# Making the high half of the gated product one column chunk later in the FFN stages

## The chip, the cores and the metric

The kernel runs on one core of one Trainium2 chip. The metric is the device time of one execution in microseconds (us), median over runs.

## What is computed

The reference is a "macaron" block on x of shape 2 x 2048 x 512 (4096 tokens), all in float32:

```
x = x + 0.5 * ffn(layernorm(x))
x = x + attention(layernorm(x))      # 16 heads of 32, causal
x = x + 0.5 * ffn(layernorm(x))

ffn(x):  w_gu, w_down = dequantised 4-bit weights (groups of 128, float16 scales)
         gate, up = x @ w_gu.T          # 1408 columns each
         h = silu(gate) * up
         y = h @ w_down.T
         return y / sqrt(mean(y*y) + 1e-6)
```

The same FFN weights are used twice.

## The kernel before

The program runs these stages: FFN, then for each of the two batches QKV projection, attention and output projection, then the FFN again. Only the FFN stages are touched by the change.

An FFN stage (class `Ffn`, `ph` 0 or 1) walks over 8 token tiles of 512 tokens (tt), and in each over 11 units (i), blocks of 128 of the 1408 gated columns. The units are numbered through, n = 11 tt + i. A unit has four chunks c, the four blocks of 128 of the 512 model columns. For each chunk two groups of two matmuls are made, up (u = 1) and gate (u = 0). The input is kept as a sum of two float16 halves x1 and x2, and each group is one weight block times x1 and times x2. The 4-bit weights have a scale for each group of 128 input columns, so each chunk's product must be scaled by itself. That is why every chunk is taken out of PSUM ("evac") rather than accumulated there:

- chunk 0, both halves: ScalarE writes `acc[u]` (a scaled copy);
- chunk 1, up: ScalarE writes a scaled copy to `tmp`, and GpSimd adds it to `acc[1]` (signal `added`);
- chunk 1, gate, and chunks 2 and 3: VectorE adds the scaled product to `acc[u]` (scalar_tensor_tensor). Chunk 2's up half has to wait for `added`.

The eight groups of a unit take their banks from a ring of four (`Ring`), so a group waits for the evacuation of the group four places before it in the ring. A "turn" (the transposition of 128 columns of the next tile's normalised input, four transposes) takes a place in the same ring.

At the end of a unit ScalarE makes silu(gate) ("silu", line 615). GpSimd multiplies it by the up half to h (lines 854 to 862; in the first tile of the first stage VectorE does this). In the next unit, h is split: ScalarE rounds it to float16, h1, the high half (line 621), and GpSimd subtracts to get h2, the low half (line 875). The down projection takes three matmuls for each 128 tokens (h1 x wd high, h1 x wd low, h2 x wd high) into four other banks Y. Its matmuls are issued LAG = 9 chunks behind, so those of unit n-1 begin in unit n+1, chunk 1.

The order of all of this is one list written by the generator `order` (line 316). Each engine's function (`ffn_pe`, `ffn_act`, `ffn_dve`, `ffn_pool`, `ffn_sp`) walks the same list and issues its own share in that order, waiting on semaphores for what it needs. An engine's queue is thus in list order, and an instruction that waits holds up all that stands behind it on its engine.

Into the list `slots` places further work: statistics of the next tile ("stat", "isd": small steps of 128x4 on VectorE in units 1 to 4), "apply" on ScalarE in units 5 and 6, the finish of the tile before ("square" on ScalarE in units 2 and 3, "rms" on VectorE in units 5 and 6, "last" on ScalarE and GpSimd in units 7 and 8), and in the units 7 to 10 the turns. The event "down" of a tile's last unit also makes ScalarE copy Y out of PSUM, which falls in the next tile's units 1 and 2. In the first tile of the first stage the weights are decoded as well: VectorE's bit operations ("decode"), TensorE's transposes, ScalarE's evacuations ("weight"), GpSimd's scaling.

In the trace nearly every instruction bears the line of a helper: L97 matmul, L100 transpose, L103 activation, L106 tensor_tensor, L109 tensor_scalar, L112 scalar_tensor_tensor. They are told apart by their operands: on ScalarE "sb<-sb 128x512 f32<-" is silu, "sb<-ps,sb" or "sb<-pp,sb" an evacuation (with its scale), "sb<-sb 128x512 f16<-" is h1, and "sb<-pp" without a scale operand a copy.

Of the kernel before, what the change touches and what calls it, by code (L numbers as in the profile page):

```python
# [281 lines left out]
class Ffn:  # L282
# [33 lines left out]
    def order(self):  # L316

        deq, ph = self.deq, self.ph
        if deq:
            yield "scales",  # L320
            yield from self.norm_v(0)
            yield from self.norm_a(0)
            yield "decode", 0, 99
            yield "scaled", 0
            yield "scaled", 1
            yield "decode", 1, 99
        for c in range(KC):
            yield "turn", 0, c
        yield "load", 1
        if deq:  # L330
            for m in range(3):
                yield "weight", m
            yield "vectors",
        for tt in range(NT):
            first = deq and tt == 0
            slots = self.slots(tt)
            for i in range(IC):
                n = tt * IC + i
                for c in range(KC):
                    for u in (1, 0):  # L340
                        yield "group", tt, i, c, u
                    for u in (1, 0) if c == 0 else (0, 1):
                        yield "evac", tt, i, c, u
                    if c == 0 and n:
                        yield "h1", n - 1
                    if c == 1 and n:
                        yield "h2", n - 1
                    d = 4 * n + c - LAG
                    if d >= 0:
                        yield "down", d // 4, d % 4  # L350
                    yield from slots.get((i, c), ())
                    if first and i + 1 < IC and c < 3:
                        yield "weight", 3 * (i + 1) + c
                    if first and c == 0 and i == 0:
                        yield "decode", 2, 99
                    if first and c and i + 3 < IC:
                        yield "decode", i + 3, 5 if c < 3 else 99
                    if tt + 1 < NT:
                        if c == 1 and i >= IC - 4 and not first:
                            yield "turn", tt + 1, i - IC + 4  # L360
                        if i == IC - 1 and first:
                            yield "turn", tt + 1, c
                if n == 0:
                    yield "settle",
                yield "silu", n
                if i == IC - 1:
                    yield "residual", tt
                    if tt + 2 < NT:
                        yield "load", tt + 2
                if tt == NT - 1 and i == 1 and ph == 0:  # L370
                    yield "ahead",
                if deq and tt in (2, 3) and i >= 3 and i - 3 + 8 * (tt - 2) < IC:
                    yield "keep", i - 3 + 8 * (tt - 2)
        n = NT * IC
        yield "h1", n - 1
        yield "h2", n - 1
        for d in range(4 * n - LAG, 4 * n):
            yield "down", d // 4, d % 4
        if ph:
            yield from self.finish_a(NT - 1) + self.finish_v(NT - 1) + self.finish_y(NT - 1)  # L380
# [1571 lines left out]
```

How the kernel before makes its waits and increments, by code:

```python
    def wait_ge(self, sem, value):  # L86
        if self.e is not None:
            assert value > 0, sem.name
            if self.seen.get(sem.name, 0) < value:
                self.seen[sem.name] = value
                self.e.wait_ge(sem, value)
# [145 lines left out]
def rsqrt_dve(e, p, out, x, scale, eps, mult, w, done=None, key=None):  # L237
    V = p.V
    v, g, t = w[:, 0, :], w[:, 1, :], w[:, 2, :]
    e.wait_ge(*V.now())
    e.tensor_scalar(v, x, scale / mult ** 2, eps / mult ** 2, ALU.mult, ALU.add).then_inc(*V.up())
    yield
    e.wait_ge(*V.now())
    e.tensor_scalar(t.bitcast(I32), v.bitcast(I32), 1, None, ALU.logical_shift_right).then_inc(*V.up())
    yield
    e.wait_ge(*V.now())
    e.tensor_scalar(g.bitcast(I32), t.bitcast(I32), -1.0, float(0x5F3759DF), ALU.mult, ALU.add).then_inc(*V.up())
    yield
    for n in range(3):
        e.wait_ge(*V.now())
        e.tensor_tensor(t, g, g, ALU.mult).then_inc(*V.up())
        yield
        e.wait_ge(*V.now())
        e.scalar_tensor_tensor(t, t, -0.5, v, ALU.mult, ALU.mult).then_inc(*V.up())
        yield
        e.wait_ge(*V.now())
        e.scalar_tensor_tensor(out if n == 2 else g, t, 1.5, g, ALU.add, ALU.mult).then_inc(
            *(done.up(key) if done and n == 2 else V.up()))
        yield
# [2 lines left out]
def norm_dve(e, p, ready, done, key, scale=1.0, eps=1e-5):  # L263
    V = p.V
    st, mv, rs, w = p.st, p.mv, p.rs, p.w4
    for tb in range(4):
        e.wait_ge(*ready)
        e.bn_stats(st[:, tb, :], p.xb[tb][:, :]).then_inc(*V.up())
        yield
```

## Time and profile before

| | |
|---|---|
| median of 3 runs | 2636.36 us (2633.56 to 2638.26) |
| the profiled execution | 2637.86 us, of which the span is 2636.0 |
| busy, share of the span | TensorE 95%, VectorE 72%, ScalarE 57%, GpSimd 56% |
| TensorE's granted clock, mean | 0.995 of full |
| HBM traffic | 38 GB/s over the span |

The span is what the trace covers; all times of rows are microseconds from its start. A row of the timeline gives start, duration, engine, line, operation, operands and number of instructions merged, and in brackets the idle time of the engine before it with the instruction that ended the wait. A duration of merged instructions reaches from the first start to the last end. The start-to-start time is the better measure for matmuls, which overlap at their ends.

### The profile page before, as it was taken

The page shows a single profiled execution, that of the slowest core. Times are in us where ns is not written, and L with a number is a line of the kernel's source. Part 1 is how long each engine was busy: PE and PEld are TensorE (multiplying, and loading weights), DVE is VectorE, ACT ScalarE, POOL GpSimd, SP SyncE. Part 2 cuts the span into 40 slices and gives each one's busy share as a digit, 9 for nine tenths or more (in the row PEclk, how much of TensorE's full clock was granted, in tenths as well). Part 3 has the DMA queues.
Part 4 walks back from the last instruction along what each step waited for, and adds up shares of the span by engine and source line. Part 5 has one row for each costly group of instructions (what it writes and reads, how often), then busy time and mean ns, then how long its engine had stood idle before and what let it go on. Part 6 is the DMA issues. An engine that isn't in the chain of part 4 may idle for free. (4 is left out here: it accounts for less than half of the span.)

```text
span 2636.0 us, 39763 instructions
## 1 busy us (share of the span) xinstructions
PE 2511.5 (95%) x14559; PEld 1060.8 (40%) x14559; DVE 1890.3 (72%) x3388; ACT 1492.3 (57%) x2861; POOL 1483.4 (56%) x1349
## 2 busy tenths in 40 slices
PE   6899999999999999999999999999999999999998
PEld 3444444444443333333344433333333444444443
DVE  7977777768668777767486687777666777777765
ACT  6666666655224666666622346666665466666664
POOL 3466666663314666667332256766673456666665
PEclk8999999999999999999999999999999999999999
DMA  2012211121122020200230310111004201111101
GB/s 65 18 47 80 81 44 45 49 96 63 34 58 60 5 50 6 66 6 3 86 124 33 90 28 19 38 31 41 4 4 164 100 17 49 48 48 49 49 33 48
DMA packets 78018, 130.58 MB, mean 50 GB/s; under 512 B 19551, under 2 KB 24698, under 8 KB 77694
## 3 DMA queue, kind: packets, MB, share of 16 engines
q1 hardware_dynamic: 77822, 128.05, 15.7%
q8 instruction: 114, 1.87, 0.3%
q14 instruction: 82, 0.67, 0.1%
HBM read 68.23 MB, written 31.46 MB: 38 GB/s over the span
## 5 line engine op out<-in xcount | busy, mean ns | idle before, releaser
L106 POOL TENSOR_TENSOR sb<-sb,sb 128x512 f32<-128x512 f32 (+6 forms) x1333 | 1475.9, 1133 | 1137.0 <-ACT sb L103 426.5
L97 PE MATMUL pp<-sb,sb 128*128 128x512 f16 (+9 forms) x11128 | 2062.8, 421 | 41.4 <-DVE sb L112 13.0
L97 PEld LDWEIGHTS pp<-sb,sb 128*128 128x128 f16 (+3 forms) x11128 | 770.0, 102 | 1119.8 <-issue 304.1
L103 ACT ACTIVATE sb<-pp 128x512 f32<-128x512 f32 (+6 forms) x1395 | 666.3, 550 | 418.5 <-PE pp L97 406.4
L97 PE MATMUL ps<-sb,sb 128*128 128x512 f16 (+6 forms) x2888 | 747.8, 346 | 51.6 <-ACT sb L103 17.5
L118 DVE TENSOR_REDUCE sb<-ps 128x1 f32<-128x512 f32 (+3 forms) x772 | 492.2, 668 | 159.2 <-PE ps L97 157.0
L103 ACT ACTIVATE sb<-sb 128x512 f16<-128x512 f32 (+5 forms) x545 | 335.8, 623 | 477.9 <-DVE sb L112 335.5
L112 DVE SCALAR_TENSOR_TENSOR sb<-ps,sb,sb 128x512 f32<-128x512 f32 x437 | 318.2, 747 | 136.7 <-PE ps L97 78.0
L97 PEld LDWEIGHTS ps<-sb,sb 128*128 128x128 f16 (+3 forms) x2888 | 247.9, 98 | 393.7 <-DVE sb L118 111.6
L112 DVE SCALAR_TENSOR_TENSOR sb<-pp,sb,sb 128x512 f32<-128x512 f32 x447 | 324.0, 745 | 84.3 <-PE pp L97 83.1
L103 ACT ACTIVATE sb<-pp,sb 128x512 f32<-128x512 f32 x325 | 218.0, 676 | 126.5 <-PE pp L97 105.0
L118 DVE TENSOR_REDUCE sb<-pp 128x1 f32<-128x512 f32 (+3 forms) x348 | 232.6, 668 | 76.9 <-PE pp L97 76.4
L103 ACT ACTIVATE sb<-ps,sb 128x512 f32<-128x512 f32 x299 | 196.8, 684 | 70.2 <-PE ps L100 66.5
L106 DVE TENSOR_TENSOR sb<-sb,sb 128x512 f16<-128x512 f32 (+5 forms) x179 | 130.3, 752 | 56.7 <-PE pp L97 53.9
L112 DVE SCALAR_TENSOR_TENSOR sb<-pp,sb 128x512 f32<-128x512 f32 (+1 forms) x88 | 60.5, 689 | 67.4 <-ACT sb L103 44.2
L115 DVE CAST sb<-sb 128x512 f16<-128x512 f32 x96 | 43.9, 459 | 69.7 <-ACT sb L103 69.6
L109 DVE TENSOR_SCALAR sb<-sb 128x384 uint16<-128x384 uint16 (+3 forms) x210 | 83.0, 413 | 9.6 <-ACT sb L103 4.0
L103 ACT ACTIVATE sb<-ps 128x512 f16<-128x512 f32 (+5 forms) x113 | 61.1, 576 | 34.9 <-PE ps L100 22.1
L112 DVE SCALAR_TENSOR_TENSOR sb<-sb 128x4 f32<-128x4 f32 x240 | 71.0, 296 | 5.7
L124 DVE BATCH_NORM_STATS2 sb<-sb 128x6 f32<-128x512 f32 x96 | 65.3, 681 | 12.1 <-DMA sb<-L_attn_X 7.0
L112 DVE SCALAR_TENSOR_TENSOR sb<-ps,sb 128x512 f16<-128x512 f32 (+1 forms) x40 | 27.5, 690 | 45.0 <-ACT sb L103 33.2
L100 PE MATMUL ps<-sb,sb 128*128 128x128 f32 x324 | 50.8, 281 | 5.7 <-ACT sb L103 3.8
(27 smaller groups left out, 365.7 us busy)
## 6 DMA issues: line engine op xcount, KB each, us to landing
sb<-sb SPq DMA_DIRECT2D x144, 128.0 KB, 2.4
sb<-L_attn_X SPq DMA_DIRECT2D x64, 256.0 KB, 3.4
sb<-xa SPq DMA_DIRECT2D x64, 256.0 KB, 4.3
sb<-xc SPq DMA_DIRECT2D x64, 256.0 KB, 3.4
xa<-sb SPq DMA_DIRECT2D x32, 256.0 KB, 2.0
xc<-sb SPq DMA_DIRECT2D x32, 256.0 KB, 4.8
out<-sb SPq DMA_DIRECT2D x32, 256.0 KB, 2.0
sb<-sb SPq DMA_DIRECT2D x48, 96.0 KB, 2.1
```

What stands on the lines that cost most here:

```text
L97: return self.e.matmul(*a, **k) if self.e else self
L100: return self.e.transpose(*a, **k) if self.e else self
L103: return self.e.activation(*a, **k) if self.e else self
L106: return self.e.tensor_tensor(*a, **k) if self.e else self
L109: return self.e.tensor_scalar(*a, **k) if self.e else self
L112: return self.e.scalar_tensor_tensor(*a, **k) if self.e else self
L115: return self.e.tensor_copy(*a, **k) if self.e else self
L118: return self.e.reduce_max(*a, **k) if self.e else self
L124: return self.e.bn_stats(*a, **k) if self.e else self
```

## The change

In `order`, the event "h1" of the unit before is yielded after the evacuations of chunk 1, where it was yielded after those of chunk 0:

```diff
                     for u in (1, 0):
                         yield "group", tt, i, c, u
                     for u in (1, 0) if c == 0 else (0, 1):
                         yield "evac", tt, i, c, u
-                    if c == 0 and n:
+                    if c == 1 and n:
                         yield "h1", n - 1
                     if c == 1 and n:
                         yield "h2", n - 1
```

The "h1" after the last unit of a stage is written separately and stays. Only ScalarE issues anything for "h1", so only its queue changes.

## Rows read from the trace of the kernel before

**Rows 1.** The page's busy time of each engine.
```profile
PE 2511.5 (95%) x14559; PEld 1060.8 (40%) x14559; DVE 1890.3 (72%) x3388; ACT 1492.3 (57%) x2861; POOL 1483.4 (56%) x1349
```

**Rows 2.** TensorE's timeline, first and last turn of the second FFN stage's first tile.
```profile
2102.18 0.60 PE L100 MATMUL ps<-sb,sb 128*128 128x128 f32 x4
...
2121.62 0.60 PE L100 MATMUL pp<-sb,sb 128*128 128x128 f32 x4
```

**Rows 3.** TensorE's timeline, second stage: a wait, first turn, last turns.
```profile
2144.05 1.04 PE L97 MATMUL ps<-sb,sb 128*128 128x512 f16 x4 [0.37 <-DVE sb L112]
...
2171.46 0.60 PE L100 MATMUL ps<-sb,sb 128*128 128x128 f32 x4
...
2192.78 0.60 PE L100 MATMUL pp<-sb,sb 128*128 128x128 f32 x4
...
2547.50 0.60 PE L100 MATMUL pp<-sb,sb 128*128 128x128 f32 x4
```

**Rows 4.** TensorE's timeline, first stage: last turns, and the start of its last unit.
```profile
198.05 0.60 PE L100 MATMUL ps<-sb,sb 128*128 128x128 f32 x4
...
552.47 0.60 PE L100 MATMUL ps<-sb,sb 128*128 128x128 f32 x4
...
619.85 0.60 PE L97 MATMUL ps<-sb,sb 128*128 128x512 f16 x2 [0.45 <-DVE sb L112]
```

**Rows 5.** The timeline in the turn stretch of the second stage's second tile.
```profile
2172.41 6.07 POOL L106 TENSOR_TENSOR sb<-sb,sb 128x512 f32<-128x512 f32 x5 [1.32 <-ACT sb L103]
...
2178.51 0.63 ACT L103 ACTIVATE sb<-sb 128x512 f16<-128x512 f32 x1 [1.18 <-POOL sb L106]
2179.05 0.67 ACT L103 ACTIVATE sb<-pp,sb 128x512 f32<-128x512 f32 x1
...
2179.77 1.25 PE L97 MATMUL pp<-sb,sb 128*128 128x512 f16 x5 [0.73 <-ACT sb L103]
```

**Rows 6.** The timeline of one ordinary unit (number 3) of that tile.
```profile
2144.68 0.63 ACT L103 ACTIVATE sb<-sb 128x512 f32<-128x512 f32 x1 [1.40 <-DVE sb L112]
...
2145.22 1.25 ACT L103 ACTIVATE sb<-ps,sb 128x512 f32<-128x512 f32 x2
...
2145.44 1.27 POOL L106 TENSOR_TENSOR sb<-sb,sb 128x512 f32<-128x512 f32 x1 [1.12 <-ACT sb L103]
2146.75 0.63 ACT L103 ACTIVATE sb<-sb 128x512 f16<-128x512 f32 x1 [0.28 <-POOL sb L106]
...
2147.29 0.67 ACT L103 ACTIVATE sb<-pp,sb 128x512 f32<-128x512 f32 x1
...
2148.03 2.39 POOL L106 TENSOR_TENSOR sb<-sb,sb 128x512 f32<-128x512 f32 x2 [1.31 <-ACT sb L103]
...
2149.34 0.75 DVE L112 SCALAR_TENSOR_TENSOR sb<-ps,sb,sb 128x512 f32<-128x512 f32 x1 [0.44 <-POOL sb L106]
...
2150.78 0.63 ACT L103 ACTIVATE sb<-sb 128x512 f32<-128x512 f32 x1 [1.40 <-DVE sb L112]
```

**Rows 7.** VectorE's small steps in the same unit, from the timeline.
```profile
2145.22 1.52 DVE L109 TENSOR_SCALAR sb<-sb 128x4 f32<-128x4 f32 x3
...
2147.53 0.35 DVE L112 SCALAR_TENSOR_TENSOR sb<-sb 128x4 f32<-128x4 f32 x2
```

**Rows 8.** First tile: busy time in 80 to 100 us by engine, then its timeline.
```profile
80.00:100.00 20.00, 14.82 (x79) 7.47 (x78) 19.61 (x44) 12.38 (x21) 8.14 (x12) 1.00 0.00 0
...
98.93 0.68 ACT L103 ACTIVATE sb<-pp,sb 128x512 f32<-128x512 f32 x1
...
99.69 2.75 POOL L106 TENSOR_TENSOR sb<-sb,sb 128x256 f32<-128x256 f32 x4 [0.46 <-ACT sb L103]
...
100.31 2.26 DVE L109 TENSOR_SCALAR sb<-sb 128x384 uint16<-128x384 uint16 x4
```

**Rows 9.** TensorE's timeline at the start of the second FFN stage.
```profile
2065.74 1.04 PE L97 MATMUL pp<-sb,sb 128*128 128x512 f16 x4 [0.95 <-ACT sb L103]
2067.87 1.46 PE L97 MATMUL ps<-sb,sb 128*128 128x512 f16 x4 [1.09 <-DVE sb L112]
```

## The prediction

> **What bounds the kernel now.** I began with the page's busy times: TensorE is busy for 95% of the span [rows 1], so only what makes TensorE wait, or keeps it from starting its next matmul on time, can be won back. The change touches the two FFN stages alone (about 35 to 625 us and 2057 to 2625 us). I then asked what TensorE would need there if nothing held it. The second FFN stage shows that by itself: in its first token tile four turns of the next tile's input follow each other at exactly 6.48 us [rows 2], one unit (one value of i) plus one turn. A turn is four transposes, 0.44 us. So a unit of 28 matmuls of 512 columns takes 6.48 - 0.435 = 6.045 us, 216 ns a matmul. A tile of 11 units and four turns then needs 11 x 6.045 + 4 x 0.435 = 68.24 us.
>
> All later tiles are slower. From the last turn of one tile to that five tiles on, the second stage takes 2547.50 - 2192.78 = 354.72 us, 70.94 a tile [rows 3]; the first stage takes 552.47 - 198.05 = 354.42 us, 70.88 a tile [rows 4]. That is 2.65 to 2.7 us over the floor in every tile, and it is all that this change can win in the regular tiles.
>
> Where does it go? One place is 0.37 us before the matmuls at 2144.05, once a tile. A second is the stretch of the turns: 2171.46 to 2192.78 is 21.32 us, where three unit periods need 19.44 [rows 3]; it loses 1.88 us, of which 0.73 stands at 2179.77 and as much again one unit later [rows 5]. The rest is spread thinly, some 0.05 us a unit.
>
> The thin loss is a loop through four engines [rows 6]. Reading down: ScalarE's silu of unit n begins at 2144.68; GpSimd multiplies it by the up half from 2145.44 to 2146.71; ScalarE rounds the product to the high half h1 at 2146.75, after 0.28 us of waiting; only then, in its own order, it evacuates chunk 1's up half to tmp (2147.29); GpSimd adds tmp at 2148.03; VectorE can then evacuate chunk 2's up half (2149.34), then chunk 3; and the next silu begins at 2150.78. The loop is 6.10 us long. It is longer than TensorE's 6.045, so once the kernel is behind it stays behind, TensorE always finding its bank 0.05 us late. The turn stretch is the same loop with more in it: there GpSimd runs five operations in a row for 6.07 us (two of them are the residual additions "last"), h1 waits 1.18 us for the product, tmp stands behind h1, and TensorE waits for exactly the bank that tmp frees [rows 5].
>
> **The change part by part.** Nothing is added or removed: the same h1 instructions, no DMA. On ScalarE alone, h1 of unit n-1 trades places with the tmp evacuation of unit n; in the units where they exist, also with the copy of Y ("down") that stood between them, and in the first tile of the first stage with one weight evacuation. SP's order is not touched. GpSimd's order stays add, h2, product.
>
> *tmp goes ahead.* After the two chunk-0 evacuations ScalarE is free at 2145.22 + 1.25 = 2146.47, and chunk 1's up group is done before that: it is matmuls 8 and 9 of the unit, so it ends 9 x 0.216 = 1.94 us after the unit's first at 2144.05, and some 0.2 us later its result can be read. So tmp moves from 2147.29 to 2146.47, 0.82 us earlier [rows 6]. GpSimd's product ends at 2146.71, and the add follows tmp by 0.74 us as now, at 2147.21. The loop without h1 is then 6.10 - 0.82 = 5.28 us if every step slides along, well under 6.045. TensorE becomes the bound in the ordinary units.
>
> *The 0.37 us once a tile* (2144.05): ScalarE has a Y copy in between here. With h1 gone from there, tmp and the add come 0.54 us earlier (the step from h1 to tmp in [rows 6], 2147.29 - 2146.75). That covers 0.37 and leaves 0.17; the prefetch of the weights wants 0.22, so perhaps 0.05 remains.
>
> *The turn stretch.* tmp of the following unit need not wait for the product at all: it can start when its group is done, 2.1 us into the unit, where TensorE wants the bank 16 matmuls and a turn after the first, at 3.9 [rows 5]. Both waits of 0.73 go. The turn's own evacuation still stands behind h1, so behind the product; but its bank is wanted only two groups later, and I count about 0.1 us of danger there. With tmp early the five GpSimd operations (6.07) fit in a unit with turn (6.48); in the last tile they face 6.045, a deficit of 0.03 a unit for two units, which the slack of the add carries.
>
> *What h1 now delays.* h2 on GpSimd stands behind the add anyway. h1 follows tmp by its 0.6 us and ends at about 2147.7, and the add ends at 2148.5: h2 does not wait for h1. The down matmuls that read h1 and h2 of n-1 come in unit n+1, chunk 1 (LAG 9). h2 is done about 5.5 us into unit n (2147.21 + 2.39 - 2144.05), the matmuls want it 11 matmuls into the next, at 6.045 + 2.37 = 8.4 us: 2.9 us of cover. If that cover were gone, each unit would stall by the excess.
>
> *What works against it.* VectorE's small 128x4 steps (inverse deviation and rms, in units 3 to 6, chunks 0 and 1) cannot run beside GpSimd: the three started at 2145.22 end at 2146.74, with GpSimd's product (2146.71); the two at 2147.53, where GpSimd is idle, take 0.35 together [rows 6, 7]. With the add moved to 2147.21 the second group falls under it and is held until 2148.48. VectorE then evacuates chunk 2 from about 4.45 us into the unit, takes 0.67 and 0.75 us for its two halves and ends the up half at 5.87, and TensorE wants that bank at 5.8 to 6.0. I charge 0.05 to 0.1 us for each of four units, so 0.3 us a tile; the ends are 0 (the prefetch absorbs it) and 0.3 a unit, 1.2 a tile.
> The Trainium skill has this as a rule (SBUF — State Buffer, section "SBUF: two separate sides"): VectorE instructions with two SBUF inputs or in a two-port mode and GpSimd's share a port pair, and whichever starts second is blocked for the whole instruction. The trace agrees with its 1.52 against 0.35 us. By the rule alone the hold would be up to one whole GpSimd operation, 1.27 us, in each of the four units, of which all but about 0.1 us lies beside TensorE's work; the sum would be the same.
>
> *First tile of the first stage* (about 35 to 130 us). Here VectorE is the bound: 19.61 of 20 us busy between 80 and 100 [rows 8]. But part of this is being held: its four bit operations of the decoding begin at 100.31 and take 2.26 us, until GpSimd's chain add, add, h2, h2 (99.69, 2.75 us) ends at 102.44. That chain starts 0.76 us after tmp (98.93), and tmp stands behind h1 (0.54 us from start to start) and a weight evacuation. With h1 behind tmp, the chain comes 0.46 us earlier, for so long GpSimd was idle before it. Nine units could win that, 4.1 us; the least is nothing, if VectorE gives it back elsewhere. I take 3.
>
> *Start of the second stage*: TensorE waits 0.95 us for tmp and then 1.09 for chunk 2 [rows 9]. tmp comes 0.94 earlier, but VectorE then has a bn_stats ahead of it; the second wait grows to about 1.4, so 0.7 is won. The granted clock is low just after (the 1.2 GHz level by the matmuls' spacing: four take 1.46 us there and 1.04 before); if the shorter wait kept it up there would be up to 1.5 us more, not counted.
>
> **The sum.**
> First stage: tile 1 like tile 1 of the second stage (2121.62 to 2192.78, 71.16, so 2.9 over), tiles 2 to 6: 354.42 - 341.2 = 13.2, last tile: from 552.47 to 619.85 is 67.38 where 0.435 + 3.02 + 10 x 6.045 = 63.91 is needed, 3.5. Together 19.6.
> Second stage: 2.9 + (354.72 - 341.2 = 13.5) + 3.5 = 19.9.
> Held small steps and remnants: 14 tiles x 0.3 = 4.2 back. First tile +3, start +0.7.
> 19.6 + 19.9 - 4.2 + 3.7 = 39.0 us.
> The profiled execution took 2637.86 us for a span of 2636.0; that gives 2598.9. It stood 1.5 us over the median of the three runs, 2636.36, so against the median I forecast 2597.4, say 2597.
>
> **The rivals.**
> 1. *The hold of the small steps is dear* (0.13). If each of the four units pays 0.3 us, and the turn's evacuation behind h1 a few tenths more, 14 x 1.5 = 21 us come back instead of 4.2, so 22.2 are won: 2636.4 - 22.2 = 2614. For it: the margin between 5.87 and 5.8 is nothing. Against it: a loop of 5.28 catches up in the next unit.
> 2. *The wait only changes its name* (0.03). If chunk 2's evacuation were late for another reason than tmp (VectorE's own queue), nothing moves: 2636. Against it: VectorE is idle for 0.4 us before it at 2149.34, put down to GpSimd [rows 6].
> 3. *Slower* (0.03). h2 reaches the down matmuls late. It decides when h2 slips by over 2.9 us; by 0.5 us more it would cost 0.5 x 154 units = 77 us, 2713. The only thing that could push it so is GpSimd in the two "last" units, where it has 6.07 us of work in 6.48; I see at most 1 us there.
> 4. *TensorE's floor is not one* (0.01). If matmuls could come closer, the new bound would be the 5.28 us loop: 0.77 x 154 = 118 us more, about 2480. Against it: ten matmuls in 2.16 us wherever nothing waits, and four turn periods equal to 0.01 us [rows 2].
> The Trainium skill speaks for this one (TensorE: Matmul & The Clock Gate, section "Back-to-back issue gap"): it gives about 131 ns a matmul of 512 columns as a sustained rate, which would be 3.67 us a unit; the same section's formula gives 216. The trace bears out the second only.
>
> My forecast's own chance is 0.80, with 2590 to 2606 as its own range (first tile 0 to 5, held steps 0 to 8). The range of the whole, 2588 to 2612, takes in most of rival 1. A measurement here tells about 0.2%, 5 us, from no change: faster 0.94, same 0.03, slower 0.03.
>
> **What would show it.** Right: in the changed kernel's ordinary units tmp follows the second chunk-0 evacuation without a gap; the turns of every tile stand at 6.48 to 6.55 instead of 7.38; a tile takes 68.3 to 68.7 us in both stages; TensorE's waits for ScalarE in the FFN stages fall from two a tile to none; h1's wait for GpSimd stays in the units after "last" but nothing of TensorE's stands behind it. Wrong: a tile over 69.5 us; a new wait of TensorE for VectorE in units 3 to 6, or for the turn's bank; any wait of a down matmul for GpSimd; a first tile that ends later than before.

## The result and the profile after

The changed kernel takes 2641.13 us in the median of 17 runs (2639.97 to 2643.96), the kernel before 2636.50 in 17 runs. The ratio is 1.002 (95% interval 1.0012 to 1.0027): slower by 4.6 us, where 39 us less had been forecast. Its profiled execution took 2639.97 us for a span of 2638.2. That is only 2.1 us more than the profiled execution of the kernel before, in which the granted clock stood below full twice where it did not here: 0.91 in 1960 to 1980 us, in the attention, and 0.93 in 2050 to 2075 us, against 1.00 in both stretches of the changed kernel.

The gain in the stretch of the turns is there to be seen. TensorE's timeline over the second tile of the second stage, from the last turn of the first tile on, answers to [rows 2, 3]:

```profile
2122.78 0.60 PE L100 MATMUL pp<-sb,sb 128*128 128x128 f32 x4
2151.05 1.04 PE L97 MATMUL ps<-sb,sb 128*128 128x512 f16 x4 [0.47 <-DVE sb L112]
2158.11 1.04 PE L97 MATMUL ps<-sb,sb 128*128 128x512 f16 x4 [0.85 <-DVE sb L112]
2164.97 1.04 PE L97 MATMUL ps<-sb,sb 128*128 128x512 f16 x4 [0.64 <-DVE sb L112]
2171.83 1.04 PE L97 MATMUL ps<-sb,sb 128*128 128x512 f16 x4 [0.64 <-DVE sb L112]
2174.86 0.60 PE L100 MATMUL ps<-sb,sb 128*128 128x128 f32 x4
2181.34 0.60 PE L100 MATMUL ps<-sb,sb 128*128 128x128 f32 x4
2187.82 0.60 PE L100 MATMUL pp<-sb,sb 128*128 128x128 f32 x4
2194.30 0.60 PE L100 MATMUL pp<-sb,sb 128*128 128x128 f32 x4
```

The turns stand 6.48 us apart, as they do in the first tile of [rows 2]; the waits of 0.73 and of 0.37 are gone. In their place are four waits for VectorE that the kernel before did not have, behind units 3, 4, 5 and 6. The tile takes 2194.30 - 2122.78 = 71.52 us. The same tile took 71.16 before and most others 70.88; here the later tiles take 71.53. Over the floor of 68.24 it loses 3.28 us: 2.60 in the four waits, and 0.17 more at each. A wait is counted from the end of the record before, and matmuls that nothing holds start some 0.16 us before that end (the row of ten matmuls at 2148.26 lasts 2.32 us, and ten starts take 2.16).

What does VectorE do in those units? Here is unit 3 of the timeline, all engines, the counterpart of [rows 6, 7]:

```profile
2145.25 1.25 ACT L103 ACTIVATE sb<-ps,sb 128x512 f32<-128x512 f32 x2
...
2145.47 1.28 POOL L106 TENSOR_TENSOR sb<-sb,sb 128x512 f32<-128x512 f32 x1 [1.15 <-ACT sb L103]
2146.51 0.69 ACT L103 ACTIVATE sb<-pp,sb 128x512 f32<-128x512 f32 x1
...
2147.28 2.38 POOL L106 TENSOR_TENSOR sb<-sb,sb 128x512 f32<-128x512 f32 x2 [0.53 <-ACT sb L103]
...
2147.61 2.06 DVE L112 SCALAR_TENSOR_TENSOR sb<-sb 128x4 f32<-128x4 f32 x2
...
2149.60 1.40 DVE L112 SCALAR_TENSOR_TENSOR sb<-ps,sb,sb 128x512 f32<-128x512 f32 x2
```

This silu begins at 2144.71, that of [rows 6] at 2144.68, so the times of the two units can be compared as they stand. tmp (2146.51) follows the chunk-0 evacuations at once and the add starts at 2147.28, both as forecast (2146.47 and 2147.21). The two small steps of chunk 1 now begin while GpSimd is at the add. Together they take 2.06 us instead of 0.35, and end at 2149.67 with h2 (2147.28 + 2.38 = 2149.66). Both evacuations of chunk 2 stand behind them, and TensorE waits for their bank at 2151.05.

The view of one source line, cut to this stretch, gives each step its own time (minimum, median, maximum in ns, then the starts of the first and the last):

```profile
L112 DVE SCALAR_TENSOR_TENSOR sb<-sb x2: 950/1014/1078, 2147.6 to 2148.6; 128x4 f32<-128x4 f32 x2
```

So neither of the two took the whole hold. The second starts at 2148.6 and ends at 2149.67, so the first took 0.95 and the second 1.08 us. The whole kernel shows the same in the page's table of groups, first before, then after:

```profile
L112 DVE SCALAR_TENSOR_TENSOR sb<-sb 128x4 f32<-128x4 f32 x240 | 71.0, 296 | 5.7
```

```profile
L112 DVE SCALAR_TENSOR_TENSOR sb<-sb 128x4 f32<-128x4 f32 x240 | 162.1, 675 | 5.7
```

The same 240 instructions take 91 us longer. VectorE's busy time rises from [rows 1] by 85 us, to 1975.1; the other engines' stay within 9 us. Here VectorE is "busy" longer with the same instructions because it is being held.

### The profile page after: what moved, and what is told of

It reads as the page before. It is cut to its first block, busy times and chain, and to the rows that moved or that the text cites. A ratio compares the mean times of both kernels' runs of the same rounds, so it can differ in the third digit from the quotient of the medians.

```text
span 2638.2 us, 39763 instructions
## 1 busy us (share of the span) xinstructions
PE 2504.1 (95%) x14559; PEld 1069.5 (41%) x14559; DVE 1975.1 (75%) x3388; ACT 1484.1 (56%) x2861; POOL 1482.8 (56%) x1349
## 3 DMA queue, kind: packets, MB, share of 16 engines
HBM read 68.23 MB, written 31.46 MB: 38 GB/s over the span
## 4 chain that ended last, share of the span: by engine, by line
PE 69%; DVE 18%; issue 4%; ACT 2%; POOL 1%; SPq 1%; DMA 0%; DVEq 0%; ACTq 0%; POOLq 0%
PE pp L97 53%; PE ps L97 15%; DVE sb L112 9%; DVE sb L118 7%; ACT sb L103 2%; POOL sb L106 1%; DVE sb L109 1%; SPq L139 1%; PE ps L100 1%; DVE sb L106 1%; PE pp L100 0%; DVE sb L115 0%; DVE sb L124 0%; DMA sb<-sb 0%; DVE sb L127 0%
## 5 line engine op out<-in xcount | busy, mean ns | idle before, releaser
L97 PEld LDWEIGHTS ps<-sb,sb 128*128 128x128 f16 (+3 forms) x2888 | 254.0, 98 | 404.6 <-DVE sb L118 111.5
L112 DVE SCALAR_TENSOR_TENSOR sb<-sb 128x4 f32<-128x4 f32 x240 | 162.1, 675 | 5.7
```

The costliest lines, as they stand in the source:

```text
L97: return self.e.matmul(*a, **k) if self.e else self
L112: return self.e.scalar_tensor_tensor(*a, **k) if self.e else self
```

## The experiments

Each kernel is the changed one with the edit shown, unless it is said otherwise; times are medians, the ratio is to the kernel before, run beside it.

**1. The small steps behind chunk 2.**

```diff
+        def w(*chunks):
+            return [(i, c) for i in chunks for c in (0, 2)]
-            place(steps[4:], v(8, 9) if first else v(3, 4), (4, 2, 4, 3))
+            place(steps[4:], w(8, 9) if first else w(3, 4), (4, 2, 4, 3))
-            place([("ahead_norm",)] * 24, v(3, 4, 7, 8, 9, 10), (2,) * 12)
+            place([("ahead_norm",)] * 24, w(3, 4, 7, 8, 9, 10), (2,) * 12)
-            place(self.finish_v(tt - 1), v(5, 6), (4, 2, 4, 2))
+            place(self.finish_v(tt - 1), w(5, 6), (4, 2, 4, 2))
```

> The changed kernel, with VectorE's small steps of chunk 1 (inverse deviation, rms, and the norm made ahead) put into chunk 2, behind its evacuations. Theory H (hold): what the change lost is that a small step started while GpSimd runs add and h2 back to back is held until both are over (2147.61 to 2149.67, with GpSimd from 2147.28 to 2149.66), 2.0 us in each of four units a tile. Behind chunk 2's evacuations, about 5.4 us into the unit, GpSimd has ended h2 (about 5.3), so the steps take their 0.35 us and lie beside TensorE's work. H: a tile 68.3 to 68.8 us, TensorE's waits of 0.48 to 0.85 gone, total 2595 to 2604. Rival W (work): those four units hold more VectorE work than fits behind the early tmp, wherever it stands. W: waits of 0.3 us or more stay in units 3 to 6, total 2620 to 2641. Rival N: the change brings nothing and something else stalls units 3 to 6: unchanged, about 2641.

2597.47 us, 0.985 (0.984 to 0.987). The timeline of unit 6 of the second stage's second tile, and the last turns of two tiles:

```profile
2143.95 2.39 POOL L106 TENSOR_TENSOR sb<-sb,sb 128x512 f32<-128x512 f32 x2 [0.45 <-ACT sb L103]
...
2146.45 0.35 DVE L112 SCALAR_TENSOR_TENSOR sb<-sb 128x4 f32<-128x4 f32 x2
```

```profile
2101.32 0.60 PE L100 MATMUL pp<-sb,sb 128*128 128x128 f32 x4
...
2169.55 0.60 PE L100 MATMUL pp<-sb,sb 128*128 128x128 f32 x4
```

GpSimd is idle from 2146.34, the steps take 0.35 us, and a tile takes 68.23 us: the floor. The total lies in H's range, the tile just under its 68.3, and TensorE has no wait left in it; W and N fall.

**2. The same move in the kernel before (h1 early): the control.** The edit is that of experiment 1, with `if c == 0 and n` for h1.

> The kernel before (h1 early), with the small steps of chunk 1 in chunk 2: the control. In the kernel before GpSimd's h2 ends at 2150.42, 0.4 us after chunk 2's up evacuation gives VectorE free (2150.01). H: the steps are held for 0.4 us, then take 0.35, and chunk 3 and the silu come 0.75 us later in four units a tile; the loop through silu, product, h1, tmp, add has no slack: 14 x 3 = 42 us slower, 2665 to 2690. W: only their own 0.35 us enters the loop, 14 x 4 x 0.35 = 20 us, 2650 to 2658. If the place of the steps does not matter: 2636.

2673.46 us, 1.014 (1.013 to 1.016): slower by 37 us. Its timeline in unit 3 and the start of unit 4:

```profile
2166.79 2.39 POOL L106 TENSOR_TENSOR sb<-sb,sb 128x512 f32<-128x512 f32 x2 [1.32 <-ACT sb L103]
...
2168.77 0.63 DVE L112 SCALAR_TENSOR_TENSOR sb<-sb 128x4 f32<-128x4 f32 x2
...
2170.79 1.69 PE L97 MATMUL pp<-sb,sb 128*128 128x512 f16 x7 [0.19 <-DVE sb L112]
```

The steps meet the end of h2 (2169.18), chunk 3's evacuations come late, and with them the banks of unit 4's chunk 1 and the next silu. The very move that repairs the changed kernel harms the old one; its cost hangs on where GpSimd is, as H says. A tile takes 73.36 us, 2.5 more than in the kernel before, and 14 x 2.5 = 35 is nearly all of the 37.

**3. All small steps in chunk 0.** The edit: counts `(6, 0, 7, 0)`, `(4, 0) * 6` and `(6, 0, 6, 0)` in the three lines, with `v` as it was.

> The changed kernel, with all small steps in chunk 0 (6 or 7 in a row) and none in chunk 1. H: the first steps are held by GpSimd's product until about 2.3 us into the unit; the five or six that remain need 0.16 to 0.19 us each, to about 3.3, but the add starts at 2.9, so the last of them is held until h2 ends (5.3). All evacuations of the unit then stand behind it and TensorE waits 1.5 to 1.7 us in each of four units a tile: slower than the changed kernel, 2660 to 2700. W (the amount of work counts, not where it stands): about the changed kernel's 2641 or a few us less, since chunk 0 has no evacuation of VectorE's.

2617.69 us, 0.993 (0.992 to 0.995). Both theories had it wrong. The timeline of unit 5, whose six small steps all stand in chunk 0:

```profile
2147.43 1.44 DVE L112 SCALAR_TENSOR_TENSOR sb<-sb 128x4 f32<-128x4 f32 x2
...
2147.58 2.38 POOL L106 TENSOR_TENSOR sb<-sb,sb 128x512 f32<-128x512 f32 x2 [0.41 <-ACT sb L103]
...
2151.11 1.04 PE L97 MATMUL ps<-sb,sb 128*128 128x512 f16 x4 [0.27 <-DVE sb L112]
```

The fifth step starts before the add and goes through. The sixth meets the add; it ends at 2148.87, when the add ends (alone it takes 1.27 us, to 2148.85), not at 2149.96 with h2. So a step is not held until GpSimd's run is over, though one held step still makes the evacuations late: a tile takes 69.76 us here. H had to be mended: a step is held by one operation only, and in the changed kernel it is the second step, which needs the first one's result, that meets the second operation.

**4. One small step in chunk 1**, to test that. Counts `(5, 1, 5, 2)`, `(3, 1) * 6` and `(5, 1, 5, 1)`.

> The changed kernel with one small step in chunk 1 and five in chunk 0 (unit 4 keeps two in chunk 1; the norm made ahead in the last tile of the first stage 3 and 1). It tells how long a held step is held. Theory S (one step, one operation): each small step is held by the one GpSimd operation that it meets, and the next step, which needs its result, meets the next operation; two steps thus cost add and h2, 2.0 us, and one costs the add alone. S: the one step of units 3, 5 and 6 ends with the add, TensorE's waits there fall to 0.1 us or none, the wait behind unit 4 stays at 0.6 to 0.9; a tile about 69.0 us, total 2606 to 2614. Theory Q (until GpSimd's run of operations is over): one step is held until h2 ends too, each of these units still loses 0.4 us or more, total 2630 to 2638.

2603.39 us, 0.987 (0.986 to 0.989). The timeline of unit 3, which has one step in chunk 1, and of unit 4, which has two:

```profile
2128.81 2.38 POOL L106 TENSOR_TENSOR sb<-sb,sb 128x512 f32<-128x512 f32 x2 [0.54 <-ACT sb L103]
...
2129.28 0.82 DVE L112 SCALAR_TENSOR_TENSOR sb<-sb 128x4 f32<-128x4 f32 x1
...
2134.85 2.39 POOL L106 TENSOR_TENSOR sb<-sb,sb 128x512 f32<-128x512 f32 x2 [0.54 <-ACT sb L103]
...
2135.32 0.82 DVE L112 SCALAR_TENSOR_TENSOR sb<-sb 128x4 f32<-128x4 f32 x1
2136.18 1.08 DVE L112 SCALAR_TENSOR_TENSOR sb<-sb,sb 128x4 f32<-128x4 f32 x1
...
2138.63 1.04 PE L97 MATMUL ps<-sb,sb 128*128 128x512 f16 x4 [0.48 <-DVE sb L112]
```

One step is let go in the middle of GpSimd's 2.38 us and costs TensorE nothing; the second of a pair is caught again and costs 0.48. S holds and Q falls; the total is 2.6 us better than S's range, and the wait behind unit 4 is 0.48, not 0.6 to 0.9. A tile takes 68.88 us, as S said. The changed kernel itself has the same picture in the last tile of its first stage, with two steps of other kinds, each under an operation of its own of GpSimd's chain:

```profile
605.25 3.61 POOL L106 TENSOR_TENSOR sb<-sb,sb 128x512 f32<-128x512 f32 x3 [0.41 <-ACT sb L103]
...
605.43 1.12 DVE L109 TENSOR_SCALAR sb<-sb 128x4 int32<-128x4 int32 x1
...
606.58 1.07 DVE L106 TENSOR_TENSOR sb<-sb 128x4 f32<-128x4 f32 x1
```

**5. Only the rms steps moved** (units 5 and 6 to chunk 2, units 3 and 4 left): the third of experiment 1's three edits alone.

> The changed kernel with only the rms steps (units 5 and 6) moved to chunk 2; those of the inverse deviation (units 3 and 4) stay in chunk 1. If the loss is a sum over units, each paying for its own held steps: the waits behind units 3 and 4 (0.48 and 0.85) stay, those behind 5 and 6 (0.64 each) go; 14 tiles x about 1.63 us less than the changed kernel's 2641, total 2616 to 2622. If the units hand lateness on, so that the first two cause the last two (one late loop): the waits behind 5 and 6 stay in part, total 2626 to 2636.

2617.79 us, 0.993 (0.992 to 0.995). TensorE's timeline of one tile:

```profile
2140.49 1.04 PE L97 MATMUL ps<-sb,sb 128*128 128x512 f16 x4 [0.49 <-DVE sb L112]
2147.55 1.04 PE L97 MATMUL ps<-sb,sb 128*128 128x512 f16 x4 [0.85 <-DVE sb L112]
2162.67 0.60 PE L100 MATMUL ps<-sb,sb 128*128 128x128 f32 x4
```

The waits of units 3 and 4 stay to 0.02 us, those of 5 and 6 are gone. Each unit pays for its own steps, and the loss adds up: the result lies 23.3 us under the changed kernel, 14 x 1.63 = 22.8 was expected.

**6. h1 late only where chunk 1 has no small steps.**

```diff
+            early = [0 if any(x[0] in ("isd", "rms", "ahead_norm") for x in slots.get((i, 1), ())) else 1
+                     for i in range(IC)]
-                    if c == 1 and n:
+                    if c == early[i] and n:
                         yield "h1", n - 1
```

> h1 late as in the change, but early (behind chunk 0) in the units whose chunk 1 carries small steps. H: the steps fall again into GpSimd's idle time between product and add and cost 0.35 us; the turn stretch keeps its 1.8 us a tile of gain, and the four early units lose 0.05 us each at most. A tile 68.3 to 68.9 us, total 2596 to 2606. W: with h1 early these four units are as in the kernel before, so the same. A rival theory G, that the late h1 gains only where the waits were (turns and the 0.37 a tile) and the thin 0.05 a unit stays: a tile 69.0 to 69.4, total 2608 to 2616.

2596.09 us, 0.985 (0.983 to 0.986). The last turns of two tiles stand 68.22 us apart:

```profile
2102.50 0.60 PE L100 MATMUL pp<-sb,sb 128*128 128x128 f32 x4
...
2170.72 0.60 PE L100 MATMUL pp<-sb,sb 128*128 128x128 f32 x4
```

G falls. Four units of the 6.10 us loop in a row (its silus at 2124.43, 2130.53, 2136.62, 2142.72 and 2148.81) do not bring TensorE to a wait: the loop before them takes 5.69, so they start early enough.

**7. h1 late only in units 8 to 10**, with `if c == (i >= 8) and n:`.

> h1 late only in units 8, 9 and 10, early in units 0 to 7. It separates the gain of the turn stretch (where h1 waited 1.2 us for GpSimd) from that of the ordinary units. If the sum of the prediction is right part by part: the two waits of 0.73 a tile go (about 1.5 to 1.9 us a tile, also in the last tiles, 14 tiles: 21 to 26 us), the 0.37 and the thin 0.05 a unit stay; no small step of units 3 to 6 meets the add. Total 2609 to 2616. If the thin loss were only a sequel of the turns' lateness, it would go as well: 2597 to 2602.

2612.68 us, 0.991 (0.989 to 0.992). One tile of TensorE's timeline:

```profile
2108.15 0.60 PE L100 MATMUL pp<-sb,sb 128*128 128x128 f32 x4
2130.55 1.04 PE L97 MATMUL ps<-sb,sb 128*128 128x512 f16 x4 [0.37 <-DVE sb L112]
2157.96 0.60 PE L100 MATMUL ps<-sb,sb 128*128 128x128 f32 x4
...
2177.75 0.60 PE L100 MATMUL pp<-sb,sb 128*128 128x128 f32 x4
```

24 us are won where 21 to 26 were expected. The 0.37 and the thin loss stay. This tile takes 69.60 us, most others 69.35, which is 1.53 less than before; twelve such tiles make 18 of the 24 us, and the second stage after its last turn takes 85.56 us instead of 88.55. The turn stretch and the ordinary units can be gained apart.

**8. The two repairs together, and experiment 6 again beside them.** `combined` is experiment 1 with `v(8, 9) if first else w(3, 4)`, and the norm made ahead in `v(3, 4, 7, 8, 9, 10), (3, 1) * 6`.

> The changed kernel with the chunk-1 small steps in chunk 2 in the regular tiles, but left in chunk 1 in the first tile of the first stage (its last turn stood at 130.69 us with the steps in chunk 2, at 128.62 in the changed kernel), and the norm made ahead in the last tile of the first stage 3 and 1 to a unit, in chunks 0 and 1 (with 2 in chunk 2 TensorE waited 1.43 and 0.55 us there, with 3 and 1 0.49). If these parts add up: 2597.5 - 2.1 - 1.5 = 2594 us, range 2592 to 2597. If they don't: 2597 to 2600.

> The kernel with h1 early only in the units whose chunk 1 carries small steps, measured again beside the combined one, to tell which of the two repairs is better: 2596 us as before, so 2 us behind the combined one if that is at 2594, equal to it if the parts do not add.

2594.89 us, 0.984 (0.983 to 0.986), and 2596.71 us, 0.985 (0.984 to 0.986). `combined` is the fastest of all, 41 us under the kernel before and 46 under the changed one; but its lead of 1.8 us over the other is less than the intervals, so whether the parts add is open.

## Why the prediction was wrong

Point by point, by its own steps:

- *The floor* of 68.24 us a tile, and the 39.5 us over it in both stages: right. The kernels of experiments 1, 6 and 8 reach 68.22 or 68.23. The rival that TensorE's floor is not one is out: with all waits of the regular tiles gone nothing came closer. The Trainium skill's 131 ns a matmul (TensorE: Matmul & The Clock Gate, "Back-to-back issue gap") differs from what is measured here, 216 ns, and the measurement decides.
- *tmp goes ahead, the 0.37, the turn stretch*: right, in the changed kernel itself and part by part in experiment 7.
- *What h1 now delays*: right. No down matmul waits for GpSimd.
- *What works against it*: **this is the step that failed.** It said that "the second group falls under it and is held until 2148.48", the end of the add, and charged 0.05 to 0.1 us a unit with 0.3 as the upper end. The group ended at 2149.67, 1.2 us later. A tile loses 3.28 us where 0.3 was charged, 0.82 a unit against an upper end of 0.3. The mechanism was named, but a pair of dependent steps was treated as one: each step is held once, and with the add and h2 back to back there is an operation for each of the two (experiments 3 and 4). The rows that the prediction used did not show this. GpSimd's product there stands alone, so of the three steps at 2145.22 [rows 7] only one could be caught, and the 1.52 us read as the hold of the group. But the kernel before has it elsewhere, in the first tile of its first stage, where GpSimd runs six operations of about 0.70 us back to back:

```profile
116.24 4.19 POOL L106 TENSOR_TENSOR sb<-sb,sb 128x256 f32<-128x256 f16 x6 [3.49 <-DVE sb L112]
...
117.66 0.84 DVE L112 SCALAR_TENSOR_TENSOR sb<-sb 128x4 f32<-128x4 f32 x2
118.53 0.65 DVE L112 SCALAR_TENSOR_TENSOR sb<-sb,sb 128x4 f32<-128x4 f32 x1
```

  The first of the three steps takes its 0.15 us as the second operation ends; the second and the third are held for 0.65 us each, to the end of one operation each.
- *The sum.* In place of 4.2 us, 47 come back: twelve tiles at 3.3 us, 4.4 and 1.5 us behind the last turn of the first and of the second stage, and 1.65 at the start of the second stage, which the prediction did not charge. This is measured against the same stretches of `combined`, the fastest kernel. By that measure the kernel before stood 40.3 us over, where 39.5 were read. With 1.2 us each from the first tile and from the start of the second stage (below), 4.5 us of loss are left; 4.6 were measured.
- *First tile*: +3 was forecast. Its last turn moved from 129.86 to 128.62 us, 1.2 us. There too more small steps are caught: four in a row from 106.18 us on, for 0.64 to 0.76 us each, where the kernel before has two (from 108.18). How much of the missing 1.8 us that is was not separated.
- *Start of the second stage*: +0.7 was forecast, and up to 1.5 more from the clock "not counted". From the first turns to the first turn in unit 7 it takes 2103.34 - 2057.16 = 46.18 us where the kernel before needs 2102.18 - 2055.67 = 46.51, though it has the first 1.65 us of held steps in it; so it is 2.0 us better apart from them. Where [rows 9] have four matmuls in 1.46 us after the second wait, the changed kernel has

```profile
2068.61 1.04 PE L97 MATMUL ps<-sb,sb 128*128 128x512 f16 x4 [1.36 <-DVE sb L112]
2069.93 1.68 PE L97 MATMUL pp<-sb,sb 128*128 128x512 f16 x7 [0.28 <-DVE sb L112]
```

The second wait grew to 1.36, as forecast (about 1.4), and the granted clock of 2050 to 2075 us is 1.00, the 2.4 GHz level, instead of 0.93. But the change did not save the clock. The kernel of experiment 7 has the order of the kernel before in these units and the same two waits, with its clock at full:

```profile
2052.99 1.04 PE L97 MATMUL pp<-sb,sb 128*128 128x512 f16 x4 [0.95 <-ACT sb L103]
2055.12 1.04 PE L97 MATMUL ps<-sb,sb 128*128 128x512 f16 x4 [1.09 <-DVE sb L112]
```

  It needs 2088.64 - 2042.92 = 45.72 us for the same stretch, 0.8 less than the kernel before. So 0.8 of the 2.0 us is the clock's fall in that one execution, and 1.2 is what the change won.

So rival 1 ("the hold of the small steps is dear", 0.13) is what happened, at more than double its price. Its upper end of 0.3 us a unit came from no row, and even at that price its 2614 us lay outside the stated 2588 to 2612, which the prediction says takes in most of it. A bound from the rows was at hand: if both steps are held to the end of h2, 2147.21 + 2.39 - 2144.05 = 5.55 us into the unit, the two evacuations (0.67 and 0.75) free the bank at 7.0 instead of 6.0. That is 1.0 us in each of four units, 56 us in 14 tiles, and 2636.4 - 43.2 + 56 = 2649: above the kernel before, and the measured 2641 inside the range.

The Trainium skill's rule (SBUF — State Buffer, "SBUF: two separate sides": of two instructions that need the shared port pair, the one that starts second is blocked for the whole of the other) agrees with every row here, taken instruction by instruction. In the changed kernel's trace 192 of the 128x4 steps start inside a GpSimd tensor_tensor that has more than 0.16 us to go, and each of them ends 0.02 or 0.03 us after that operation. The prediction applied the rule once to a group of two.

## What to carry to other kernels

When a transfer of order moves long work of one engine, list what small instructions of other engines now start under it, and count them one by one. A chain of n small steps, each of which needs the one before, beside n back-to-back long operations of the engine that holds it can cost n long operations, not one (two in the changed kernel's later tiles; steps that do not depend on each other were not tried). Look for the idle gap of that engine in the new timetable and put the chain there; the place that was free in the old timetable is the wrong one in the new (experiments 1 and 2: the same move, 44 us to the good and 37 to the bad). And when a change that should pay comes out even, compare the busy times of the same instructions before throwing it away.

## What the runs showed of the hardware

- VectorE's 128x4 steps with all operands in SBUF take 0.16 us when GpSimd is idle. When they start during a GpSimd tensor_tensor of 128x512 they last until it ends, so up to 1.26 us by what is left of it (0.95 and 1.08 in the changed kernel's unit 3, 0.82 in experiment 4, 1.26 for the sixth step in experiment 3), for scalar_tensor_tensor, tensor_tensor and int32 tensor_scalar alike. The evacuations, which read PSUM, take 0.75 us at either time.
- Between two back-to-back operations of GpSimd a waiting step of VectorE does get through (experiment 4: 0.82 us, let go in the middle of 2.38), and GpSimd's pair takes the same 2.38 or 2.39 us with one step, two or none waiting.
- A loop through four engines that is 0.05 us longer than TensorE's own unit costs nothing for four units if TensorE's banks are early at its start (experiment 6), and 0.05 us a unit once they are late, as in the kernel before.
